# Edge layer of a graph network: one-hot comparisons made in two halves, with a scan step between the halves

## The reference

```python
h = jnp.maximum(_layernorm(x, axis=-1), 0.0)
x_i, x_j = h[dst], h[src]
e = jax.nn.relu(jnp.concatenate([x_i, x_j - x_i], axis=-1) @ W1 + b1)
out = jax.ops.segment_max(e @ W2 + b2, dst, num_segments=12500)
x = x + jnp.where(jnp.isfinite(out), out, 0)
```

## Time and profile before

| | us |
|---|---|
| median of 3 runs | 18585.29 (18583.72 to 18618.24) |
| span of the profiled execution | 13809.8 |
| VectorE busy in the span | 9045.7 (66%) |
| GpSimd busy | 7815.4 (57%) |
| TensorE matmul busy | 7082.0 (51%) |
| ScalarE busy | 5948.2 (43%) |
| comparisons of all stages' 128x2048 form, L685 | 2201.7 in 2000, mean 1.101 |

### The profile page before, as it was taken

The page is one execution under the profiler, slowest core; times in us unless marked ns, Lnnn a source line. Parts: engine busy times, 40 slices in busy tenths (PEclk is TensorE's granted clock), DMA queues, the critical chain, the costliest instruction groups (busy, mean ns, idle before and its releaser), DMA issues. The chain is left out here.

```text
span 13809.8 us, 283975 instructions
## 1 busy us (share of the span) xinstructions
PE 7082.0 (51%) x96792; PEld 5084.7 (37%) x96792; DVE 9045.7 (66%) x17848; ACT 5948.2 (43%) x10705; POOL 7815.4 (57%) x7194
## 2 busy tenths in 40 slices
PE   2266666666666663998899999700000000000066
PEld 1155555555555552554455555400000000000055
DVE  5388888888888886444444344466666666666585
ACT  0144444444444443776777677522222222222201
POOL 5677777777777773111111111367777777777700
PEclk9866666666666666999899899755555555555598
DMA  7333333333333333886688588422222222222197
GB/s 308 144 112 113 112 114 114 119 112 112 113 112 115 115 114 94 261 265 220 200 263 267 172 265 263 160 72 66 63 66 66 66 63 66 63 63 66 60 361 241
DMA packets 1274431, 1981.83 MB, mean 144 GB/s; under 512 B 256937, under 2 KB 987918, under 8 KB 1268737
## 3 DMA queue, kind: packets, MB, share of 16 engines
q1 hardware_dynamic: 867553, 1059.78, 24.4%
q10 hardware_dynamic: 174288, 612.09, 12.0%
q0 software_dynamic: 231664, 297.80, 8.1%
HBM read 1167.21 MB, written 815.55 MB: 144 GB/s over the span
## 5 line engine op out<-in xcount | busy, mean ns | idle before, releaser
L632 POOL DMA_INDIRECT RF<-tab_edge_b,idx x3125 | 3541.2, 1133 | 1030.6 <-issue 948.6
L1180 POOL DMA_INDIRECT records<-RF,idx x3125 | 3130.6, 1002 | 984.5 <-issue 984.5
L1737 ACT ACTIVATE X<-bk 128x392 uint8<-128x392 f32 x4000 | 1782.6, 495 | 1565.0 <-PE bk L1898 1548.0
L685 DVE TENSOR_TENSOR HM<-iota_b,eqw 128x2048 bf16<-128x2048 bf16 x2000 | 2201.7, 1101 | 342.7 <-PE bk L1898 197.6
L1898 PE MATMUL bk<-HM 128*64 128x98 bf16 x32000 | 1583.2, 247 | 1306.7 <-ACT X L1737 672.8
L1898 PE MATMUL kp<-HM,ident_b 128*64 128x98 bf16 x6250 | 281.7, 283 | 3805.4 <-DVEq L1646 3805.4
L876 POOL DMA_INDIRECT agg<-RF,lastT x372 | 536.9, 1443 | 2856.9 <-ACT RF L808 2766.0
L769 PE MATMUL tp<-HM,RF 128*64 128x512 bf16 x12276 | 2001.2, 379 | 7.9 <-ACT HM L728 2.0
L1898 PEld LDWEIGHTS bk<-HM 128*64 128x64 bf16 x32000 | 1239.8, 134 | 1653.2 <-issue 1571.3
L1898 PEld LDWEIGHTS kp<-HM,ident_b 128*64 128x64 bf16 x6250 | 261.7, 168 | 3826.3 <-issue 3826.3
L775 PE MATMUL om<-HM,RF 128*64 128x512 bf16 x6138 | 1442.3, 379 | 0.0
(11 more groups left out here) (362 smaller groups left out, 14805.4 us busy)
## 6 DMA issues: line engine op xcount, KB each, us to landing
dst_f<-counts SPq DMA_DIRECT2D x465, 512.0 KB, 4.6
RF<-first_rows SPq DMA_DIRECT2D x250, 800.0 KB
counts<-X ACTq DMA_DIRECT2D x250, 784.0 KB
records<-RF ACTq DMA_DIRECT2D x88, 1960.0 KB, 8.2
RF<-records SPq DMA_DIRECT2D x220, 784.0 KB
crow<-counts SPq DMA_DIRECT2D x279, 512.0 KB, 4.7
first_rows<-RF ACTq DMA_DIRECT2D x25, 4000.0 KB, 49.5
edge_rows<-RF ACTq DMA_DIRECT2D x125, 800.0 KB, 8.0
```

Of the source, the lines that this page charges most:

```text
L632: e.indirect_dma_start(out=ring[:, r, j, :], out_offset=None, in_=table[:, :], in_offset=bass.IndirectOffsetOnAxis(ap=idx[:, r, j:j + 1], ...
L685: return e.tensor_tensor(to[:, 0:n, :].rearrange("p k (q h) -> p k q h", h=2), iota_b[:, 0:m].rearrange("p (q h) -> p q h", h=2).unsqueeze ...
L1180: e.indirect_dma_start(out=records[:, :], out_offset=bass.IndirectOffsetOnAxis(ap=idx2[:, r, j:j + 1], axis=0), in_=msgs[MSG_OF[r]][:, j, ...
L1737: e.activation(staged[u].rearrange("p (r k) -> p r k", k=P)[:, :, k:k + 4], bk[s % 2][:, 0:4 * TILES].rearrange("p (k r) -> p r k", k=4), ...
```

## The change

Every comparison of the histogram parts and of the count batches is issued as two comparisons, each over half of the edges (8 and 8, or 4 and 5), and yields after each. The step pattern is changed so that the number of scan steps for a pair stays as it was: one fill step a yield in place of two, and in batches 1 to 7 one maximum step a yield, with a fill step after it at every first half. `batched` is raised by the last half of the second comparison. Nothing else differs; the other engines' programs are the same.

```diff
+            def halves_of(oh, twice, m, last):
+                n = twice.shape[1]
+                for a, c in ((0, n // 2), (n // 2, n)):
+                    ins = row_onehots(e, oh[:, a:c, :], twice[:, a:c, :], m)
+                    if last and c == n:
+                        ins.then_inc(sem("batched"), 1)
+                    yield
+
             def hist_batch(b, h):
                 wait(e, "banked", b * CW - (4 if h == 0 else 0))
                 gate(e)
                 for oh, a, m in ((ohq, 0, P), (ohr, 1, TILES)):
-                    last = row_onehots(e, oh[h], lane_keys[:, a, HIST[h].start:HIST[h].stop, :], m)
-                    if a == 1:
-                        last.then_inc(sem("batched"), 1)
-                    yield
+                    yield from halves_of(oh[h], lane_keys[:, a, HIST[h].start:HIST[h].stop, :], m, a == 1)
...
-                    last = row_onehots(e, oh[v % 2], kb[:, r % 2, a, v * VS:(v + 1) * VS, :], m)
-                    if a == 1:
-                        last.then_inc(sem("batched"), 1)
-                    yield
+                    yield from halves_of(oh[v % 2], kb[:, r % 2, a, v * VS:(v + 1) * VS, :], m, a == 1)
...
                 for h in range(2):
                     for _ in hist_batch(b, h):
-                        several(filling, 2)
+                        several(filling, 1)
                 for _ in count_batch(b, r, 0):
-                    several(filling, 2)
+                    several(filling, 1)
...
-                        for _ in count_batch(b, r, v):
+                        for n, _ in enumerate(count_batch(b, r, v)):
                             several(taking, 1)
-                            several(filling, 1)
-                            several(taking, 1)
+                            if n % 2 == 0:
+                                several(filling, 1)
```

## The result

Measured beside each other, the changed kernel takes 18,696 us (18,676 to 18,713), the kernel before 18,601 us (18,584 to 18,618): ratio of the medians 1.0052, interval 1.0039 to 1.0064; applied to 18,601 us that is +97 us (73 to 119). The forecast was 18,719 us, +134 us on 18,585.

The account below looks back on a forecast made before the run. VectorE's instruction order was taken to set the edge-layer block period, with TensorE's counting before batch 0. 121 us from batch 1 on plus 13 us before gave +134 us on 18,585, so 18,719 us; range 18,630 to 18,810.

Parts of the forecast that it names:

- 4,775.5 us lie outside the span: Whole kernel: the gap between profile span and median time was taken as fixed, and the span's change added to the median.
- the tail: Batch 1 to the block's end: fourteen added comparisons on VectorE's path, +0.97 us a block, 121 us.
- the head: Block up to batch 1's start: +0.14 us on average in 100 blocks, -0.05 in 25, together about 13 us.
- The fixed part: VectorE comparisons: each added one costs 0.069 us, read from start-to-start pitches; twenty make +1.38 us a block.
- (2): Rival, VectorE: no change, a small half's fixed part near 0.04 us equals the stall removed; 18,585 +/- 37 us; chance 0.08.
- (3): Rival, VectorE: faster, an added instruction costs less than 0.039 us; 18,487 us at most, 18,549 likelier; chance 0.05.
- (4): Rival, VectorE: each added instruction costs the durations' full fixed part, 0.14 us; +350 us, 18,935 us; chance 0.05.
- TensorE's release: Histogram part 0: the comparison that releases TensorE ends 0.21 us later, moving batch 0 by +0.21 us.
- Rival (1): Head of block: TensorE's part does not bite, the pairs' stall returns in full; +75 us, 18,660 us; chance 0.12.
- Batch 1's start: Count batches 0 to 1: start moves by +0.08 or +0.21 us, +0.14 on average, in blocks inside a loop body.
- rival 5: GpSimd becomes the bound through longer gathers; at a tenth of a microsecond each 18,875 us; chance 0.06.
- The signal coming 0.39 us closer to the next batch: From batch 1 on: does not bite; without cover, each of seven batches would add up to 0.39 us.

Follow-up runs that it names:

- e10: The kernel before, unchanged, profiled at the slower operating point: 18,443 us.
- e1: The kernel before, unchanged, profiled once more: 13,818 us, with the kernel before at 13,828 us beside it.
- e5: The changed kernel, unchanged, timed again against the kernel before at 13,818 us: ratio 1.0105, +145 us.
- e4: Comparisons in quarters in batches 1 to 7 alone, the rest as in the kernel before: ratio 1.0277, +383 us.
- e12: The kernel before with 13 of the 25 row gathers of an edge-layer block, at 13,834 us: ratio 0.9991, -12 us.
- e2: Halves in count batches 1 to 7 alone, the rest as in the kernel before, at 13,828 us: ratio 1.0106, +147 us.
- e3: Halves in the two histogram parts and batch 0 alone, the rest as in the kernel before: ratio 1.0009, +12 us.
- e7: The kernel before without halves, fill steps reordered so the signal to TensorE comes 0.52 us earlier, at 18,622 us: ratio 1.0011, +20 us.

## Why the prediction was right, and where not

**The base was read wrongly.** "4,775.5 us lie outside the span ... I take those 4,775.5 us as they are" is false. At the 18.5 ms point they lie inside the span: the kernel before has 8117 us of edge loop there (e10) against 4676 (e1), and nearly all of the other 1,180 us is in the last layer. Span and time of one run differ by 2 us. The direction and the range survived because a longer tail costs about the same at both points. That was luck: nothing in the prediction looked at a block with a wait of 30 us, and such a wait could have hidden the tail as it hides the head.

**The sum came right by two errors that cancel.** Means a block at the 13.8 ms point, kernel before and changed kernel (e5): the tail goes from 26.70 to 27.35 us, +0.65 where the sum had 0.97; the head from 10.95 to 11.51, +0.56 where it had 0.10. Together +1.21 against 1.07. In microseconds of the kernel that is about 81 and 70 in place of 121 and 13. So the total speaks less for the working than it seems to. The terms one by one:

**The fixed part, 0.069 us, held.** In e5 the pitches of 1024, 784 and 392 elements are 0.61, 0.47 and 0.27 us, where the line through the larger sizes gave 0.605, 0.479 and 0.274. e4 gives 0.067 from the measured times alone. Rivals (2), (3) and (4) needed 0.04, under 0.039 and 0.14.

**The tail, +0.97 us a block.** Batch 1 to the end of the block is 4120.34 to 4146.90 = 26.56 us in e5, 25.79 in the earlier trace rows: +0.77. The missing 0.20 us are in batches 3, 5 and 7, which start behind VectorE's wait for its own maximum step. There a whole comparison takes 1.21 us to its first step in the kernel before, 0.06 to 0.07 more than elsewhere:

```profile
4018.01 1.28 DVE L685 TENSOR_TENSOR HM<-iota_b,eqw 128x2048 bf16<-128x2048 bf16 x1 [0.52 <-PE bk L1898]
4019.22 0.27 DVE L1393 SCALAR_TENSOR_TENSOR RF<-RF,dupjunk,om 128x64 f32<-128x64 f32 x1
```

A half takes 0.61 (the same three batches in e5, medians), so three surcharges go. The surcharge comes with GpSimd's gathers. In e12, where they end early, batch 3 has 1.20 us in the 91 blocks with a gather beside it and 1.14 in the 22 without, and batches 5 and 7, without one in every block, have 1.14. At the 18.5 ms point no gather runs there, the whole comparison takes 1.15 (3035.60 to 3036.75 in e10), no surcharge goes, and the tail grows by 0.98 us. With 0.19 us for the surcharges added back, the medians of e2 (+0.77) and e4 (+2.74) give 0.069 and 0.070 us for each added comparison (an estimate for e4, where I take it that its quarters lose the same three). The mean of the tail grows by less, 0.65, because in the block before a loop turn most of the growth vanishes in the turn's wait (30.05 and 30.15 us).

The product 125 x 0.97 = 121 us stands against +147 us (124 to 167) measured for e2. By its profile the tail is only about half of that, +0.61 us a block on the mean; +0.58 us is in the head, which its edit didn't touch. Half of that is in the block after a loop turn, whose head goes from 12.6 to 14.1 us. The prediction has no term for this, a longer tail that makes the next head longer; why it does stays open.

**TensorE's release, +0.21 us, held to the hundredth.** In e5 the releasing half ends at 4113.74, 2.84 us after the block's first comparison, and batch 0 starts at 4116.86, 3.12 us after that, as in the earlier trace rows. The wait grew from 0.38 to 0.81 us; I had said about 0.9. That is why e3 gains nothing: what the four pairs ahead of batch 0 give back (0.52 us, less 0.28 for four added comparisons) turns into a longer wait. Rival (1) is dead. One thing was left out: in the 25 blocks after a loop turn I took the later release for hidden (-0.05 us). There batch 0 starts 6.15 us after the release on the mean, before it was 4.93 (in the other blocks 3.12 and 3.05).

**Batch 1's start was put too early.** I took -0.13 us for batch 0 where VectorE sets batch 1, and +0.14 us for both together. In e5 batch 1 waits for om in 114 of 118 blocks, not in 50 of 121, and starts 3.47 us after batch 0 where it was 3.26 before (medians inside a loop body; on the mean of all blocks 3.49 and 3.43). The step mis-sized is the cover of the product in om: +0.06 us on the mean in place of -0.08, some 17 us. The granted clock of the stage is 0.67 in place of 0.68; that this is the cause I haven't shown.

**At the point where the record was measured,** +97 us (73 to 119), the tail is in, +0.98 us in ordinary blocks and 0.4 in those before a loop turn, 108 us in all. The head's cost vanishes in the 30 us wait, less a little that batch 0's halves give back behind it (-0.13 x 125 = -16 us by the same pitches). 92 us is within the interval. But the two profiles, e10 and the changed kernel's, are from different times and perhaps chips, and their heads differ by more than all this (39.58 and 40.44 us): with no pair of profiles from one chip this sum is argued, not shown.

**GpSimd (rival 5)** is out at the 13.8 ms point, for the kernel before by e12, for the changed one because GpSimd still waits for VectorE. Its waits for the index lists grew as predicted, to 115.4 us only, not to many times 34.9.

**The signal coming 0.39 us closer to the next batch did not bite:** waits between batches stayed at 0.5 us (332 waits, 171.0 us, now put down to VectorE's own step).

**Slips in the working.** The list that leads to 2.84 us names four scan steps, the sum has three, which is right. "It waits only for TensorE" leaves out VectorE's waits for its own mask steps, 47.8 us from 690 to 5300 us. And the 1.101 us in the table of the profile before is the mean over 1000 comparisons of 2048 elements (1.239 us) and 1000 of 1568 (0.963), not of one form. Nothing hangs on these.

## What to carry to other kernels

Read the cost of one more instruction from start-to-start pitches at several sizes, not from durations: here a line through three sizes priced pieces of less than half the smallest to 0.01 us. A stall removed in front of a wait for another engine is not a gain; what counts there is the signal that ends the wait (e7 moved it earlier, but was measured only where 30 us of other waiting hide it). And check that the span of the profile and the timed median belong together before using one for the other: here a gap of thousands of microseconds was a second operating point, not time outside the span. And a total that comes out right is no proof of its terms: here the tail was put half too high and the head far too low.

## What the runs showed that was not expected

The same program runs at 13.8 ms on chips 6 and 10 (on 10 in two measurements an hour apart) and at 18.5 or 18.6 ms on chips 2 and 13. At the slower point TensorE receives single matmuls in steps of some 0.7 us, for 30 us a block, while GpSimd's gathers run back to back at 1.25 us each (mean duration 0.97 us, against 1.136 at the other point). The stretch ended 4.3 us after the last gather in the block shown (3079.59 and 3083.92), and VectorE's work then follows the gathers instead of overlapping them. What feeds TensorE so slowly stays open: the one experiment for it ran on a chip without the effect.

A comparison of 2048 elements that starts behind VectorE's wait for its own last step takes 0.06 us longer when a gather of GpSimd runs beside it; a half of it shows nothing of the kind, 0.609 us with gathers beside it (e5) and without (the changed kernel's first profile).
